# Two fp32 towers on one core: attention's first weights are split in the chunk before attention, TensorE's drains are left out, and the large buffers start at multiples of 512 bytes

## The reference, cut to what matters

```python
def enc(W1, b1, g, be, W2, b2):                      # er_* gives sr, ei_* gives si
    h = gelu(_ln(x @ W1.T + b1, g, be))              # x: 1024 x 2048, W1: 2048 x 2048
    return (h @ W2.T + b2).reshape(Bsz, N, D)        # 4 states of 512
qr, kr, vr = sr @ Wq_r.T + bq_r, ...                 # and qi, ki, vi of si
w = softmax(sqrt(ar**2 + ai**2 + 1e-08) * HD**-0.5)  # over the 4 states, 8 heads
attn_r = (w @ vr) @ Wo_r.T + bo_r                    # and attn_i
R = attn_r @ int_Wr - attn_i @ int_Wi                # per state, and I
...                                                  # phases, superposition, its norm
amp = sqrt(mr**2 + mi**2)
z = gelu(_ln(amp @ post_W.T + post_b, ...))
y = relu(relu([z, x] @ W_top1 + b_top1) @ W_top2 + b_top2) @ W_top3
```

## Time and profile before

| what | us |
|---|---|
| median of 3 runs | 3156.53 |
| lowest and highest | 3155.43, 3160.82 |
| the profiled execution's own time | 3158.42 |
| its span, first to last instruction | 3156.2 |
| PE busy (share of the span) | 2994.1 (95%) |
| DVE busy | 1571.9 (50%) |
| ACT busy | 1112.7 (35%) |
| POOL busy | 232.9 (7%) |

### The profile page before, as it was taken

The page is one execution under the profiler, slowest core; times in us unless marked ns, Lnnn a source line. Parts: engine busy times, 40 slices in busy tenths (PEclk is TensorE's granted clock), DMA queues, the critical chain, the costliest instruction groups (busy, mean ns, idle before and its releaser), DMA issues. The chain is left out here.

```text
span 3156.2 us, 43886 instructions
## 1 busy us (share of the span) xinstructions
PE 2994.1 (95%) x15808; PEld 2575.5 (82%) x15808; DVE 1571.9 (50%) x2819; ACT 1112.7 (35%) x1873; POOL 232.9 (7%) x241
## 2 busy tenths in 40 slices
PE   8999999999699999999969999999999989999798
PEld 7888888888588877888869999999999977777686
DVE  3222222212531125221156766767767658999973
ACT  3111111111331114211144555555555554555553
POOL 1000000000110111110100000000000001112000
PEclk9999999999899999999989999999999989999899
DMA  5222222221442334332252232232232374444410
GB/s 201 74 76 73 73 75 74 64 59 60 151 143 76 100 93 140 104 99 75 85 174 68 54 87 73 57 96 60 66 93 53 91 178 92 102 94 90 138 46 11
DMA packets 364351, 285.47 MB, mean 90 GB/s; under 512 B 280192, under 2 KB 280320, under 8 KB 364160
## 3 DMA queue, kind: packets, MB, share of 16 engines
q1 hardware_dynamic: 341632, 206.97, 24.5%
q0 software_dynamic: 22656, 77.67, 7.1%
HBM read 194.40 MB, written 90.18 MB: 90 GB/s over the span
## 5 line engine op out<-in xcount | busy, mean ns | idle before, releaser
L50 PE MATMUL banks<-a_whi,a_xhi 128*128 128x512 f32 x1152 | 449.8, 390 | 17.9 <-DVE a_wlo L167 11.4
L52 PE MATMUL banks<-a_whi,a_xlo 128*128 128x512 f32 x1152 | 448.7, 390 | 0.0
L51 PE MATMUL banks<-a_wlo,a_xhi 128*128 128x512 f32 x1152 | 448.6, 389 | 0.0
L50 PE MATMUL banks<-b_ghi,b_whi 128*128 128x512 f32 x1024 | 402.1, 393 | 10.6 <-DVE b_slo L377 9.5
L52 PE MATMUL banks<-b_ghi,b_wlo 128*128 128x512 f32 x1024 | 399.3, 390 | 0.0
L51 PE MATMUL banks<-b_glo,b_whi 128*128 128x512 f32 x1024 | 399.3, 390 | 0.0
L167 DVE TENSOR_TENSOR a_wlo<-a_wraw,a_whi 128x512 fp32r<-128x512 f32 x144 | 99.6, 691 | 576.9 <-ACT a_whi L153 576.9
L153 ACT ACTIVATE a_whi<-a_wraw 128x512 fp32r<-128x512 f32 x144 | 90.9, 631 | 667.2 <-PE banks L52 628.3
L50 PE MATMUL banks<-t_sx,s_whi 128*128 128x256 f32 x1024 | 293.3, 286 | 28.0 <-DVE s_wlo L1257 24.0
L362 DVE TENSOR_TENSOR b_wlo<-b_wraw,b_whi 128x512 fp32r<-128x512 f32 x128 | 88.1, 690 | 446.3 <-ACT b_whi L314 446.1
L52 PE MATMUL banks<-t_sx,s_wlo 128*128 128x256 f32 x1024 | 290.0, 283 | 0.0
(11 more groups left out here) (156 smaller groups left out, 5558.1 us busy)
## 6 DMA issues: line engine op xcount, KB each, us to landing
a_wraw<-w_first SPq DMA_DIRECT2D x144, 256.0 KB, 2.6
b_wraw<-w_second SPq DMA_DIRECT2D x128, 256.0 KB, 2.6
t_sx<-s_scr SPq DMA_DIRECT2D x64, 512.0 KB, 4.4
a_scr<-t_at SPq DMA_DIRECT2D x256, 128.0 KB, 2.1
s_axng<-a_scr SPq DMA_DIRECT2D x64, 512.0 KB, 6.0
s_wraw<-w_pieces SPq DMA_DIRECT2D x82, 256.0 KB, 4.3
h_scr<-a_hst POOLq DMA_DIRECT2D x72, 256.0 KB, 2.7
b_hl<-h_scr POOLq DMA_DIRECT2D x16, 1024.0 KB, 5.9
```

Source lines behind the costliest of these rows:

```text
L50: mm(out, ahi, bhi, start=first, stop=False)
L51: mm(out, ahi, blo, start=False, stop=False)
L52: return mm(out, alo, bhi, start=False, stop=last)
```

## The change

It does four things.

1. The drains of the first and the second layers are left out. `w_used` is counted for all steps of a chunk but the last (15 or 7 a chunk instead of 16 or 8); split 3 of a chunk waits for `bank_full` (or `acc_full`) of the chunk before instead.
2. The split buffers of the states' stage become common to all stages: g.hi and g.lo, 32 rows of 512 each, with g.wraw over g.lo, hold xhi and xlo, then ghi and glo, then attention's weights. ids, emb and k01 become common too.
3. In the last chunk of the second layers SyncE loads pieces 0 to 23 into rows that are used up, four after each step (and from the ninth on only when the piece 8 before is split), and ScalarE and VectorE split pieces 0 to 15, behind their last own split and ahead of the last chunk's evacuation. The states' stage loads from piece 24 on and splits from piece 16 on.
4. `align(512)` puts padding ahead of the large buffers; ohi, olo and at move ahead of the small softmax buffers. In the states' stage hi, lo, sx and what lies over it, qs, ks, v, ptl, ohi, olo and at then start at multiples of 512 bytes.

```diff
+    def align(self, to):
+        at = -(-(PARTITION - self.nc.sbuf_bytes_remaining) // 32) * 32
+        if at % to:
+            self.sb(f"pad{at}", [P, (to - at % to) // 4])
...
-        xhi = s.sb("xhi", [P, KI, TOK], F32R)
-        xlo = s.sb("xlo", [P, KI, TOK], F32R)
+        xhi, xlo = (t[:, :, :].rearrange("p (k a) w -> p k (a w)", a=2) for t in (g.hi, g.lo))
+        s.align(512)
...
             def w_high(c, k):
                 act.wait_ge(w_loaded[k % RAW], c * (16 * KI // RAW) + 16 * (k // RAW + 1))
-                act.wait_ge(w_used, c * KI + (k + 1))
+                if k >= SPL:
+                    act.wait_ge(w_used, c * (KI - 1) + (k - SPL + 1))
+                elif zeroth(c):
+                    pass
+                elif k < SPL - 1:
+                    act.wait_ge(w_used, c * (KI - 1) - (SPL - 2 - k))
+                else:
+                    act.wait_ge(bank_full, c * TT)
...
-                        if k == KI - 1 and t < TT - 1:
+                        if k == KI - 1:
                             m.then_inc(bank_full, 1)
                     if k < KI - 1:
                         m.then_inc(w_used, 1)
-
-                m.then_inc(bank_full, 1)
-                pe.drain().then_inc(w_used, 1)
...
+            for i in range(24):
+                if i % 4 == 0:
+                    sp.wait_ge(w_used, (2 * CH - 1) * (ST - 1) + (i // 4 + 1))
+                if i >= TR:
+                    sp.wait_ge(g.w_split, i - TR + 1)
+                sp.dma_start(g.wraw[:, i, :], g.w_pieces[i]).then_inc(g.w_loaded[i % TR], 16)
...
+            def next_high(n):
+                for i in range(n):
+                    act.wait_ge(g.w_loaded[i % TR], 16 * (i // TR + 1))
+                    act.activation(g.hi[:, i, :], g.wraw[:, i, :], ACT.Copy).then_inc(g.w_hi, 1)
...
                 for j in range(AHEAD, ST):
                     w_high(br * CH + (CH - 1), j)
+                if br == 1:
+                    next_high(16)
                 s_high(br, CH - 1)
...
+                if br == 1:
+                    next_low(16)
                 s_low(br, CH - 1)
...
-                if j == ST - 1:
-                    pe.drain().then_inc(w_used, 1)
-                else:
+                if j < ST - 1:
                     mm.then_inc(w_used, 1)
...
-            for i in range(NP):
+            for i in range(24, NP):
                 piece(i)
...
-            pieces(0, M_V * KD)
             blocks(act, block_body)
...
-            pieces(0, M_V * KD)
             blocks(dve, block_body)
```

More of the change, by code:

```diff
@@ L25 @@
 TT = TOK // P
+PARTITION = 224 * 1024 - 32
 BT = 64
@@ L33 @@
 SPL = 4
+TR = 8
 COL_B2 = 4 * KI
@@ L52, in split3, with zeroth @@
     return mm(out, alo, bhi, start=False, stop=last)
+def zeroth(c):
+    return isinstance(c, int) and c == 0
 class Stage:
@@ L203, in _ @@
         def _(pe):
-            pe.sem_inc(w_used, SPL)
             pe.sem_inc(bank_read, TT)
@@ L233, in phase_second_layers @@
     with s.ctx:
-        ghi = s.sb("ghi", [P, KI, TOK], F32R)
-        glo = s.sb("glo", [P, KI, TOK], F32R)
+        ghi, glo = (t[:, :, :].rearrange("p (k a) w -> p k (a w)", a=2) for t in (g.hi, g.lo))
+        s.align(512)
         wraw = s.sb("wraw", [P, RAW, W])
@@ L312, in w_high @@
                 act.wait_ge(w_loaded[j % RAW], c * (16 * ST // RAW) + 16 * (j // RAW + 1))
-                act.wait_ge(w_used, c * ST + (j + 1))
+                if j >= SPL:
+                    act.wait_ge(w_used, c * (ST - 1) + (j - SPL + 1))
+                elif zeroth(c):
+                    pass
+                elif j < SPL - 1:
+                    act.wait_ge(w_used, c * (ST - 1) - (SPL - 2 - j))
+                else:
+                    act.wait_ge(acc_full, c * 4)
                 act.activation(whi[:, j % SPL, :, :].rearrange("p a n -> p (a n)"), wraw[:, j % RAW, :],
@@ L337, in _ @@
                         act.wait_ge(g_split, br * KI + (k + 1))
-                        if k == 0:
-                            act.wait_ge(w_used, br * (CH * ST) + SPL)
+                        if k == 0 and br > 0:
+                            act.wait_ge(acc_full, br * (CH * 4))
                         act.activation(gf[:, k % 2, :], g.ps[:, 2 * (k % 2):2 * (k % 2) + 2, :].rearrange("p a n -> p (a n)"),
@@ L364, in w_low, with next_low @@
                                   ALU.subtract).then_inc(w_split, 1)
+            def next_low(n):
+                for i in range(n):
+                    dve.wait_ge(g.w_hi, i + 1)
+                    dve.tensor_tensor(g.lo[:, i, :], g.wraw[:, i, :], g.hi[:, i, :].bitcast(F32),
+                                      ALU.subtract).then_inc(g.w_split, 1)
             def chunk_bias(cc):
@@ L491, in phase_states @@
     NP = 8 * KD
-    TR = 8
     M_Q, M_K, M_V, M_O = 0, 2, 4, 6
@@ L502, in phase_states @@
     with s.ctx:
[L503 to L510, removed]
+        ids, emb, k01 = g.ids_sb, g.emb, g.k01
+        whi, wlo = g.hi, g.lo
+        wraw = g.wraw
         turns = ExitStack()
@@ L525, in phase_states @@
         ptl = sb_t("ptl", [P, 2, W])
+        ohi = sb_t("ohi", [P, KD, 2, C], F32R)
+        olo = sb_t("olo", [P, KD, 2, C], F32R)
+        at = sb_t("at", [P, 2, 2, 2, C], F32R)
+        thi, tlo = at[:, 0], at[:, 1]
         mg2 = sb_t("mg2", [P, KD, GH, N])
@@ L532, in phase_states @@
         tinv = sb_t("inv", [P, KD, GH])
[L533 to L536, removed]
         turns.close()
@@ L604, in phase_states @@
         a_stored = [s.sem(f"t_stored{i}") for i in range(2)]
-        w_loaded = [s.sem(f"w_loaded{i}") for i in range(TR)]
-        w_hi = s.sem("w_hi")
-        w_split = s.sem("w_split")
+        w_loaded, w_hi, w_split = g.w_loaded, g.w_hi, g.w_split
         ids_in = s.sem("ids_in")
@@ L700, in phase_states @@
         B_SUP, B_M, B_POST, B_TOP1, B_TOP2 = 0, 2, 4, 5, 6
-        def zeroth(t):
-            return isinstance(t, int) and t == 0
         def done_units(t, n):
@@ L1832, in build @@
         g.tiny_hd = ctx.enter_context(nc.sbuf_tensor("tiny_hd", [P, 1], F32))
+        s = Stage(nc, "g")
+        ctx.enter_context(s.ctx)
+        g.ids_sb = s.sb("ids", [P, TT, N], mybir.dt.int32)
+        g.emb = s.sb("emb", [P, TT, N * N])
+        g.k01 = s.sb("k01", [P, 2])
+        s.align(512)
+        g.hi = s.sb("hi", [P, 2 * KI, W], F32R)
+        with nc.sbuf_tensor("g_wraw", [P, 2 * KI, W], F32) as g.wraw:
+            pass
+        g.lo = s.sb("lo", [P, 2 * KI, W], F32R)
+        g.w_loaded = [s.sem(f"w_loaded{i}") for i in range(TR)]
+        g.w_hi = s.sem("w_hi")
+        g.w_split = s.sem("w_split")
         with nc.sbuf_tensor("stats", [P, CHUNKS_A * TT, 6], F32) as g.stats:
```

## The result

| what | before | after |
|---|---|---|
| median (us) | 3156.99 of 4 runs | 3120.68 of 4 runs |
| lowest and highest | 3155.43, 3160.82 | 3116.82, 3122.73 |
| the profiled execution's own time | 3158.42 | 3116.82 |
| its span | 3156.2 | 3115.2 |
| PE busy (share of the span) | 2994.1 (95%) | 2981.3 (96%) |

The ratio is 0.9885, with an interval of 0.9872 to 0.9897: 36.3 us less by the medians, 41.6 by the profiled pair (the profiled execution of the changed kernel is the shortest of its four). 3119 was forecast. `split3` now has the lines L52 to L54, where before it had L50 to L52.

A forecast was written before the change was run, and what follows sets the result against it. TensorE was taken to bound attention and nearly fill the layers, VectorE to bound the interaction. Drains 21.4, early weights 10.3 and alignment 5.3 us made 37.0 off 3158.4, or 3119 after adjusting to the runs' median; range 3110 to 3128.

The forecast's parts named there:

- Drains: First and second layers: without the drains, chunk boundaries lose their idle, 8.5 and 12.9 us, together -21.4 us.
- the rival that gave it 7 us: First and second layers: the jump back itself costs 0.4 us on 18 jumps, giving 3126; chance 0.10.
- No idle of TensorE before L50 but at the start of branches: Sign at chunk boundaries of the first and second layers: steps of 0.23 us, TensorE idle only where branches start.
- Weights early: Passage from second layers to attention: TensorE waits for the states alone, -10.3 us, bounds -9 and -11.
- Alignment: V's projection -4.7 us and the interaction's first tile -0.6 us from aligned stationary operands, Q and K 0: -5.3 us.
- For Q and K no aligned row exists ... I take 0: Attention's Q and K: alignment taken as no change, with +4 us and -4 us as bounds.
- by other than -0.3: Sign in attention: the prediction is wrong if blocks of 57.7 us change by anything but -0.3 us.
- Alignment gives nothing or costs Q and K: Attention: no gain gives 3124.3, Q and K at 119.9 ns as well 3123 to 3128; time 3125, chance 0.20.
- an off stationary operand costs 6.1 ns a matmul, an off moving one nothing visible: Matmul steps: a stationary operand off 64-byte lines costs 6.1 ns a matmul, an off moving one nothing visible.
- Transfers: Passage to the interaction: aligned 256-byte runs might need one transaction instead of two; the sum takes 0.
- The rival that gave 5 us for it: Passage to the interaction: waits of 15.0 us on transfers shrink by half, -5 us, so 3114; chance 0.10.
- The slower rival: Attention: TensorE's two reads fall into step, 13 ns more on every 256-column matmul, +60 us, so 3179; chance 0.02.

The follow-up runs named there:

- weights late: The changed kernel with the early loads and splits taken out, so pieces 0 to 15 are loaded and split in the states' stage again: 3131.78 us, ratio 0.9928.
- old offsets: The changed kernel with hi, lo, sx, ax, ng, ohi, olo and at back at their earlier offsets from 512 bytes: 3152.26 us, ratio to before 0.9991.

## Why the prediction was right, and where it was not

*Drains.* Forecast 8.5 and 12.9 us. The pair of traces shows 8.6 and 13.7, putting them back costs 9.3 and 12.7 in the trace and 21.6 in the median. The jump back costs nothing by itself: the step across it is the usual 0.227 now (272.21 to 272.43), as in attention's loop; the rival that gave it 7 us is out. "No idle of TensorE before L50 but at the start of branches" (L52 now) came true.

*Weights early.* Forecast 10.3. The stop is 9.4 us shorter, the start comes 5.55 us behind the issue (5.4 forecast), and the splits end 5.3 us before their deadline (4 to 5 forecast). 22 cold matmuls had been expected again; only some 16 came (half speed up to 1583.3 instead of 1618.3), 0.6 us better. The mechanism held; the term was too small. Taking it back costs 11.1 us by the medians, 13.6 by the ratios and 13.6 in the trace: beside the stop, attention was 3.4 us shorter from its first to its last Q, K or V matmul, of which 0.7 was forecast (the second stop) and the 13 equal blocks explain next to nothing, and the passage to the interaction 1.0 shorter (43.7 before, 42.7 after). With the weights late 2.3 and 0.9 of that are lost again. In the passage the mean granted clock was 0.84 with 43.6 and 43.7 us (weights late, before) and 0.88 with 42.7 (after, old offsets).

*Alignment.* Here the forecast's size failed. V did nearly what was forecast (-5.4 ns on 768 matmuls, -4.1 us, where 4.7 was forecast). The step that failed is "For Q and K no aligned row exists ... I take 0": they went to 119.9, the upper bound, 3,072 x 1.2 ns = +3.7 us, and a block stayed at 57.73 where 57.4 was forecast. The prediction called itself wrong if the blocks changed "by other than -0.3"; that point was wrong, and the rival "Alignment gives nothing or costs Q and K" named what happened. Its 3125 was not seen: the median of 3120.7 lies between it and the forecast. The forecast also read the rows in too simple a way: "an off stationary operand costs 6.1 ns a matmul, an off moving one nothing visible". The runs show that neither buffer's own address counts but the distance of the two.

The interaction's first tile took 48.0 instead of 49.8 us; but in the experiments it took 46.0 to 50.6 with nothing of it changed, and 47.5 with the old offsets. None of its 1.8 us can be put down to alignment.

*Transfers.* Aligned runs of 256 bytes do land sooner: loads of ax after 5.1 to 5.4 us and stores of at after 1.9 in all kernels where these buffers lie at multiples of 256, and after 5.9 to 6.0 and 2.1 where they lie at 64, 128 or at the old offsets. The Trainium skill, "DMA: Bandwidth & Descriptors", section "How a descriptor splits into AXI transactions", says that an AXI transaction must start from a 256-byte-aligned address. For a descriptor of 256 bytes that makes two transactions instead of one when it starts elsewhere; the prediction's wording was too general, since a short one that stays within its 256 bytes needs no second. The landings agree in direction, and no run here shows the transactions. For the time it came to nothing: from attention's last Q, K or V matmul to the interaction's first the old offsets took 42.7 us and the changed kernel 42.7 too. The rival that gave 5 us for it is out.

*The slower rival* had two read streams fall into step and cost 13 ns. That the distance matters was right; but distance 0 is the good one for 512 columns, and what it costs Q and K is 1.2 ns against their distance before, not 13.

*The sum.* It came out 1.7 us from the median, and part of that is luck. Alignment, forecast at 5.3 us, gave about 0.4 in attention (4.1 less 3.7); with that alone put right the forecast would have been 3124. It was made up by parts for which less or nothing was forecast. From stage to stage the pair of traces differs by 1.9 us before the first matmul, 8.6 and 13.7 in the layers and 0.3 between them, 9.4 at the stop, 3.4 in attention, 1.0 in the passage, 1.7 in the interaction and 1.2 behind it. The 1.9 us at the start are chance: the first matmul is at 9.55 us instead of 11.43, and between 9.1 and 12.0 in the other kernels, which start with the same work. The interaction's part is less than its first tile varies by (above). What was undone adds up to 21.6 + 11.1 = 32.7 us of the 36.3 by the medians, and to 23.7 + 13.6 = 37.3 by the ratios; the two differ because the kernel before was itself 2.4 us faster beside the experiments, and neither leaves a remainder that is clear of the 6 us between the lowest and the highest run of the changed kernel.

## What to carry to other kernels

A drain at the end of a loop's body cost about a microsecond a turn here (0.9 us of idle and 0.1 in the matmul behind it) even with nobody waiting for it, and a count on the last matmul does the same work; look for rows of a loop without one to price it. When a buffer is shared between stages, check its offset against every operand that it meets in each stage: here 320 bytes cost 30 us in the two stages that the alignment seemed not to concern. And for the step of a matmul it is the distance of the stationary and the moving operand modulo 256 bytes that has to be chosen, not alignment as such: 0 for 512 columns, 192 for 256 columns here.

## What the runs showed of the hardware that was not expected

- fp32r matmuls, 128 x 128 stationary, the moving start less the stationary start modulo 256 bytes. 512 columns: 226.7 ns at 0 (V 228.0 to 228.3, with the same 227 in the middle and some steps of 231 to 236); 228.9 to 229.2 at 64; 232.4 to 233.3 at 128; 233.2 to 233.3 at 192. At 32 and 224, where one operand starts off a multiple of 64, 233.2 (V with sx at 480 and at 32); 233.4 at 96 (V before). 256 columns: 119.9 at 0, 117.3 at 32, 117.8 at 64, 114.2 to 114.7 at 192, 118.3 at 224; at 96 the output projection had 119.9, at 160 Q and K 118.3 to 118.7. Each of the 256-column values but those at 0 and 192 is from one kind of matmul. What happens inside was not tried; that the next weights are read while the moving operand streams is in every trace (a weight load beside each matmul), and is only a likely cause.
- At distance 0 nearly every step of 256 columns is 120 ns sharp in the changed kernel. With the same mean the output projection's steps were scattered over 116, 121 and 125 ns before (distance 96), and over 117 to 125 in the kernel with sx alone at 192, where its own distance is 0; so the neighbours may matter too, which was not tried. A mean within 1 ns can hide different patterns.
- A transfer in runs of 256 bytes lands about 0.7 us later in the median (5.9 to 6.0 us instead of 5.1 to 5.4, loads of ax) if its buffer in SBUF lies 64, 128 or 224 bytes past a multiple of 256.
